# A decoder's grouped-query cross attention on one core: running maxima held in bf16, column sums and three of fifteen key tiles of a pass multiplied as bf16 halves

## The reference, cut to what matters

```python
q = rope(rms_norm((x @ Wq.T).reshape(b, 256, 16, 128)))
kv_in = concat([context, x], axis=1)                      # 1857 rows
k = rope(rms_norm((kv_in @ Wk.T).reshape(b, 1857, 4, 128)))
v = (kv_in @ Wv.T).reshape(b, 1857, 4, 128)
scores = einsum('bhqd,bhkd->bhqk', q, repeat(k, 4)) * 128 ** -0.5
attn = einsum('bhqk,bhkd->bhqd', softmax(scores), repeat(v, 4))
x = x + attn.reshape(b, 256, 2048) @ Wo.T
```

## Time and profile before

| what | value |
|---|---|
| median of three runs | 1650.81 us (1650.22 to 1650.82) |
| the profiled execution | 1648.11 us, its span 1646.3 us |
| PE busy | 1470.2 us (89%), 8223 matmuls |
| DVE busy | 1287.7 us (78%) |
| POOL busy | 1127.9 us (69%) |
| ACT busy | 1029.3 us (63%) |
| mean granted TensorE clock | 0.966 of full speed |

### The profile page before, as it was taken

The page is one execution under the profiler, slowest core; times in us unless marked ns, Lnnn a source line. Parts: engine busy times, 40 slices in busy tenths (PEclk is TensorE's granted clock), DMA queues, the critical chain, the costliest instruction groups (busy, mean ns, idle before and its releaser), DMA issues. The chain is left out here.

```text
span 1646.3 us, 25844 instructions
## 1 busy us (share of the span) xinstructions
PE 1470.2 (89%) x8223; PEld 855.8 (52%) x8332; DVE 1287.7 (78%) x2581; ACT 1029.3 (63%) x2439; POOL 1127.9 (69%) x1033
## 2 busy tenths in 40 slices
PE   6598697757778999999999999989999999999988
PEld 5477365533544555455455555545545555554455
DVE  7876577878569888787977888887887878878766
ACT  3364464744366777676677766676776766766552
POOL 2363471112459789988978998888898878877742
PEclk9799798979899999999999999999999999999999
DMA  3000831020000001000000100000000000000020
GB/s 102 1 2 2 296 114 39 1 73 0 32 1 14 14 1 41 14 1 1 1 1 1 28 14 1 1 1 1 14 28 1 1 1 1 1 1 1 1 59 26
DMA packets 30991, 38.47 MB, mean 23 GB/s; under 512 B 4996, under 2 KB 26504, under 8 KB 30856
## 3 DMA queue, kind: packets, MB, share of 16 engines
q1 hardware_dynamic: 30856, 36.82, 6.9%
HBM read 35.76 MB, written 1.05 MB: 22 GB/s over the span
## 5 line engine op out<-in xcount | busy, mean ns | idle before, releaser
L2168 POOL TENSOR_TENSOR stream_acc<-stream_acc,stream_weights 128x512 f32<-128x512 f32 (+1 forms) x374 | 491.9, 1315 | 80.6 <-ACT stream_weights L2059 59.0
L1988 PE MATMUL stream_banks<-stream_weights,stream_v 128*128 128x512 f32 (+1 forms) x876 | 451.6, 600 | 0.0
L2240 DVE TENSOR_TENSOR stream_most<-stream_most,stream_banks 128x512 f32<-128x512 f32 (+1 forms) x416 | 284.9, 685 | 157.4 <-ACT stream_weights L2053 142.2
L2053 ACT COPY stream_weights<-stream_banks 128x512 f32<-128x512 f32 (+1 forms) x438 | 256.6, 586 | 238.8 <-PE stream_banks L1956 231.0
L2059 ACT ACTIVATE stream_weights<-stream_weights 128x512 f32<-128x512 f32 (+1 forms) x438 | 278.5, 637 | 60.2 <-DVE stream_weights L2226 57.6
L2226 DVE TENSOR_TENSOR stream_weights<-stream_weights,stream_banks 128x512 f32<-128x512 f32 (+1 forms) x438 | 297.0, 680 | 2.8 <-PE stream_banks L1977 1.5
L2175 POOL TENSOR_TENSOR stream_by_cos<-stream_by_cos,stream_by_sin 128x256 f32<-128x256 f32 x192 | 135.8, 728 | 88.4 <-DVE stream_by_sin L2282 88.2
L1956 PE MATMUL stream_banks<-stream_q_t_lo,stream_k_t_hi 128*128 128x512 bf16 (+1 forms) x479 | 181.7, 379 | 9.2 <-DVE stream_most L2240 3.1
L1956 PE MATMUL stream_banks<-stream_q_t_hi,stream_k_t_lo 128*128 128x512 bf16 (+1 forms) x480 | 182.1, 379 | 0.1
L1956 PE MATMUL stream_banks<-stream_q_t_hi,stream_k_t_hi 128*128 128x512 bf16 (+1 forms) x388 | 147.6, 381 | 15.5 <-DVE stream_most L2240 14.8
L1988 PEld LDWEIGHTS stream_banks<-stream_weights,stream_v 128*128 128x128 f32 (+1 forms) x876 | 144.0, 191 | 29.7 <-issue 5.3
(11 more groups left out here) (445 smaller groups left out, 3099.6 us busy)
## 6 DMA issues: line engine op xcount, KB each, us to landing
memory_raw_t<-in_ctx_t SPq DMA_DIRECT2D x4, 1601.0 KB, 9.1
memory_raw<-in_ctx SPq DMA_DIRECT2D x4, 1536.0 KB
row_ctx_t<-in_ctx_t SPq DMA_DIRECT2D x6, 512.0 KB, 3.7
early_raw<-in_L_xattn_Wq SPq DMA_DIRECT2D x4, 512.0 KB, 3.8
early_raw<-in_L_xattn_Wo SPq DMA_DIRECT2D x4, 512.0 KB, 3.9
row_ctx_t<-in_ctx_t SPq DMA_DIRECT2D x1, 1601.0 KB, 7.0
moe_raw_up<-in_L_ffn_wi SPq DMA_DIRECT2D x6, 256.0 KB, 4.3
model_x<-in_x SPq DMA_DIRECT2D x1, 1024.0 KB, 5.4
```

The source lines that it names most:

```text
L1988: nc.tensor.matmul(ps[:, 2 + n, :], v[0:r, g % 2, t, :], room(step)[0:r], start=(t == 0), stop=(t == KT - 1)).then_inc(weighed, 1)
L2053: nc.scalar.copy(room(step)[0:r], ps[0:r, step % 2, :]).then_inc(copied, 1)
L2168: nc.gpsimd.tensor_tensor(acc[0:r, h % 2, :], acc[0:r, h % 2, :], room(step)[0:r], ALU.add).then_inc(acc_ready, 1)
L2240: nc.vector.tensor_tensor(most[0:r], most[0:r], ps[0:r, step % 2, :], ALU.max).then_inc(maxed, 1)
```

## The change

The maxima, the exponentials, the sums and the rest stay where they are; what differs:

- `most` is bf16, and PE turns it with bf16 transposes into the first half of bank 6 read as bf16.
- `turn_top`, `flatten`, `own` and its DMA are gone. In slot 1, after `lower`, DVE makes `tops`, the bf16 identity times `top` (`place_top`, 128x512), and in slot 2 PE spreads it with one bf16 product of 512 columns against an array of -1 (`less`).
- Column sums: in slot 6 ACT casts `acc` to a bf16 half, DVE subtracts it to make the other (`split_high`, `split_low`, into `halves`, part of the array `raw`), and PE makes eight bf16 products of one column in slot 7 instead of eight f32 records in slot 6. The last pass keeps the f32 way.
- Key tiles 5, 10 and 14: 19 slots after its scores the exponentiated tile is split in the same way into the same two `halves`, and 20 slots after `weigh` makes three bf16 products of halves of v and p. v of these tiles is kept as two bf16 halves in the room of the f32 tile; ACT writes the one, DVE the other.
- A split waits until PE has used the split before it. In a slot DVE makes `split_low` after `keep_most`, and ACT makes `split_high` after `exponent`.
- `raw` is shared, so Wo is loaded in eight parts of 256 KB, the context chunks 2 and 3 being issued behind parts 5 and 6.

```diff
-TOPS_LATE, FLAT_LATE, SPREAD_LATE = STEPS, STEPS + 1, STEPS + 2
+TOPS_LATE, SPREAD_LATE = STEPS, STEPS + 2
 SUM_LATE = ATT_LATE + 1
+SPLIT_LATE = SUM_LATE
+SPLIT_TILES = (5, 10, 14)
+def sums_in(slot):
+    return [h for h in pass_at(slot, SUM_LATE + 1) if h < PASSES - 1] + [h for h in pass_at(slot, SUM_LATE) if h == PASSES - 1]
+def splits_in(slot):
+    found = [("sum", h) for h in pass_at(slot, SPLIT_LATE) if h < PASSES - 1]
+    step = slot - LOWER - 1
+    if 0 <= step < ALL and step % STEPS in SPLIT_TILES:
+        found.append(("tile", step))
+    return found
...
-        most = sb("most", [P, HALF])
+        most = sb("most", [P, HALF], BF16)
+        tops = sb("tops", [P, 4, P], BF16)
+        turned_most = ps[:, 6, :].bitcast(BF16)[:, 0:HALF]
+        raw_o = raw[:, 0:512].rearrange("p (h n) -> p h n", h=2)
+        halves = [raw[:, 512 + 256 * i:768 + 256 * i].bitcast(BF16) for i in range(2)]
...
                 def out_weights(k):
                     if k >= 1:
-                        sp.wait_ge(wo_lo, 2 * k)
+                        sp.wait_ge(wo_lo, k)
...
-                        last = nc.tensor.transpose(ps[:, 6, c * P:(c + 1) * P], most[:, c * P:(c + 1) * P], const["ident"][:])
+                        last = nc.tensor.transpose(turned_most[:, c * P:(c + 1) * P], most[:, c * P:(c + 1) * P], const["ident_b"][:])
-                def turn_top(h):
-                    pe.wait_ge(top_ready, h + 1)
-                    wait_bank6("flat", h)
-                    nc.tensor.matmul(ps[0:4, 6, 0:P], top[:], const["ident_b"][:], start=True, stop=True).then_inc(top_turned, 1)
                 def spread(h):
-                    pe.wait_ge(flat_ready, h + 1)
+                    pe.wait_ge(tops_ready, h + 1)
...
-                    for c in range(4):
-                        last = nc.tensor.matmul(ps[:, 7, c * P:(c + 1) * P], own[:, c, :], flat, start=True, stop=True)
-                    last.then_inc(spread_ready, 1)
+                    nc.tensor.matmul(ps[:, 7, :], less[:], tops[:].rearrange("p c n -> p (c n)"), start=True, stop=True).then_inc(spread_ready, 1)
...
+                    if t in SPLIT_TILES:
+                        if n == 0:
+                            pe.wait_ge(taken, part_at[(UNITS * g + QT + t // 4, t % 4 // 2)] + 1)
+                        pe.wait_ge(split_lo, split_at["tile", step] + 1)
+                        for one, two in ((0, 0), (0, 1), (1, 0)):
+                            last = nc.tensor.matmul(ps[:, 2 + n, :], value_halves(g, t)[one][0:r], halves[two][0:r],
+                                                    start=False, stop=(t == KT - 1 and one == 1))
+                        last.then_inc(weighed, 1)
+                        return
...
-                        pe.wait_ge(acc_ready, after_first(STEPS * (h + 1) - 1))
+                        pe.wait_ge(split_lo, split_at["sum", h] + 1)
                         for c in range(4):
-                            last = nc.tensor.matmul(ps[:, 6, c:c + 1], acc[:, h % 2, c * P:(c + 1) * P], ones[:], start=True, stop=True)
+                            for part in range(2):
+                                last = nc.tensor.matmul(ps[:, 6, c:c + 1], halves[part][:, c * P:(c + 1) * P], ones_b[:],
+                                                        start=(part == 0), stop=(part == 1))
...
+                def split_high(kind, n):
+                    if kind == "sum":
+                        ac.wait_ge(acc_ready, after_first(STEPS * (n + 1) - 1))
+                    else:
+                        ac.wait_ge(p_ready, n + 1)
...
+                    nc.scalar.copy(split_part(kind, n, 0), split_source(kind, n)).then_inc(split_hi, 1)
...
+                def place_top(h):
+                    ve.wait_ge(top_ready, h + 1)
+                    if h >= 1:
+                        ve.wait_ge(spread_ready, h)
+                    nc.vector.tensor_tensor(tops[:], bcast(const["ident_b"][:], 1, 4), bcast(top[:], 2, P), ALU.mult).then_inc(tops_ready, 1)
...
+                def split_low(kind, n):
+                    ve.wait_ge(split_hi, split_at[kind, n] + 1)
+                    nc.vector.tensor_tensor(split_part(kind, n, 1), split_source(kind, n), split_part(kind, n, 0), ALU.subtract).then_inc(split_lo, 1)
```

More of the change, by code:

```diff
@@ L1843, in cross_stream @@
         for s in SLOTS:
-            for kind, items in (("tops", pass_at(s, TOPS_LATE)), ("flat", pass_at(s, FLAT_LATE)), ("turn", turns_in(s)),
-                                ("sum", pass_at(s, SUM_LATE)), ("out", outs_in(s))):
+            for kind, items in (("tops", pass_at(s, TOPS_LATE)), ("turn", turns_in(s)),
+                                ("sum", sums_in(s)), ("out", outs_in(s))):
                 for item in items:
@@ L2028, in _ @@
                         turn_most(h)
[L2029 to L2030 removed]
                     for u in turns_in(slot):
                         turn(u)
[L2033 removed]
+                    for h in sums_in(slot):
                         sum_up(h)
@@ L2084, in take_values @@
                         ac.wait_ge(weighed, STEPS * (HALVES * (g - 2) + 1) + tiles.stop)
-                    nc.scalar.copy(v[:, g % 2, tiles.start:tiles.stop, :], projected_values(u, n)).then_inc(v_taken, 1)
+                    plain = [t for t in tiles if t not in SPLIT_TILES]
+                    for t in tiles:
+                        if t in SPLIT_TILES:
+                            last = nc.scalar.copy(value_halves(g, t)[0], projected_values(u, n)[:, t - tiles.start, :])
+                    if plain:
+                        last = nc.scalar.copy(v[:, g % 2, plain[0]:plain[-1] + 1, :],
+                                              projected_values(u, n)[:, plain[0] - tiles.start:plain[-1] + 1 - tiles.start, :])
+                    last.then_inc(v_taken, 1)
                 def high(u):
@@ L2113, in _ @@
                         exponent(slot - LOWER)
+                    for kind, n in splits_in(slot):
+                        split_high(kind, n)
                     for h in pass_at(slot, ATT_LATE):
@@ L2126, in _ @@
                             vary(u, 1)
-                    for h in pass_at(slot, FLAT_LATE):
-                        flatten(h)
                     for u in turns_in(slot):
@@ L2319, in _ @@
                         lower(slot - LOWER)
+                    for h in pass_at(slot, TOPS_LATE + 1):
+                        place_top(h)
                     for h in pass_at(slot, ATT_LATE + 1):
@@ L2330, in _ @@
                         keep_most(slot)
+                    for kind, n in splits_in(slot):
+                        split_low(kind, n)
                     if 0 <= slot - WEIGH < ALL:
                         accumulate_rest(slot - WEIGH)
-                    for h in pass_at(slot, SUM_LATE):
+                    for h in sums_in(slot):
                         invert(h)
```

81 lines of the change are left out of this document (44 added, 37 removed).

## The result

The changed kernel takes **1751.95 us** (median, 1749.73 to 1754.25) against 1650.78 (1650.22 to 1650.82) of the kernel before, run beside it: **1.0614 times as long**, 95% interval 1.0595 to 1.0632. The forecast had the sign; its +26 us are +101, outside the range of 1625 to 1702. The profiled execution has a span of 1751.4 us against 1646.3, so the two traces hold 105.1 us of difference.

What follows compares the result with a forecast made beforehand. PE was taken to bound plain passes, DVE and POOL the long ones. Plain pairs +1.3 us (+21 in all), long passes +6, start and end −1 on 1648.1 gave 1674, as median 1677; range 1655 to 1702 for this case, 1625 to 1702 overall.

Steps and rivals of the forecast that it cites:

- W: Time one split_low holds DVE: 0.6 to 1.6 us, taken as 1.0, and as 1.2 for the even pass's sum split.
- Sum split, even pass, +2.4: Even pass: PE waits for the sum's low half, so slot 8's scores start 2.4 us later; bounds 1.8 to 2.8.
- odd pass, +0.3: Odd pass: the sum's split makes slot 8 start 0.3 us later; bounds 0 and 0.9.
- some 3: Even pass: PE, reaching the sums at about 1295.1, stands some 3 us waiting for the split.
- What a wait costs: Sum splits in plain passes: PE's wait was charged as the delay to slot 8, 2.4 us even and 0.3 odd.
- The renewing passes, "1.3 each, +6": Five long passes renewing context and rotation tables: 1.3 us added to each (five POOL waits at 0.3), +6 in all.
- Tile splits, "0.5 a pair": Tile splits in slots 3, 9 and 14: delay add_out and the second Wo projection, 0.5 us a pair; bounds 0 and 2.
- 12.5 free: DVE in a plain pair: 12.5 us free of 67.3, in 16 pieces, against ten added instructions of 10 us.
- Start and end, "−1": Stage start and last pass: constant's wait and cast, turn_top and flatten go, three splits come; −1 us together.
- PE's saving, 1.30 a pass: PE's cheaper weigh, turning, turn_top and sums save 1.30 us a pass, 42 in 32, if PE stayed the bound everywhere.
- The saving arrives: Rival: quicker bf16 maxima free DVE about 4 us a pass, so no wait at the sums; 1626 us; chance 0.25.
- POOL becomes the bound: Rival: POOL pays 1.0 us per added DVE instruction, even passes stretch some 1 us; 1700 us; chance 0.10.

Runs made afterwards that it cites:

- kernel 3: Changed kernel without the tile splits: all fifteen tiles weighed in f32, sums from bf16 halves kept; 1709.2 us, 1.0361.
- Kernel 1: Changed kernel with the row sums taken as before, in f32 in slot 6 without a split; tile splits and bf16 maxima kept; 1688.9 us, 1.0238.
- experiment 4: Changed kernel with twelve more bf16 products on PE in even passes, ahead of its wait for the sum's low half; 1736.4 us, 1.0526.
- kernel 5: Changed kernel with only the maxima's part (bf16 maxima and turning, place_top, single spread product); sums and all tiles f32, Wo in eight parts; 1640.5 us, 0.9948.
- experiment 6: kernel 5 plus ACT and DVE making the halves for tiles 5, 10 and 14, which nobody reads; 1693.4 us, 1.0266.
- experiments 3 and 7: 3 made kernel 3; 7 is kernel 5 plus ACT and DVE making halves of the sum in slot 6 that nobody reads, 1643.2 us, 0.9969.

## Why the prediction was wrong in size

By its own steps, with what was measured:

- **W, DVE's time for a split: right on average, wrong where it was used.** The 87 tile splits take 1.00 us by record on average. But the sum's split, for which 1.2 stood, takes 0.69 by record in all eight plain even passes, and DVE's next instruction starts 0.60 after it (1370.51 to 1371.11), the lower bound. In kernel 3, without tile splits, it takes 1.35 in all eight.
- **Sum split, even pass, +2.4; odd pass, +0.3: right, in part by luck.** Kernel 1 differs from the changed kernel in the sums alone: most of its plain even passes take 32.3 us and its shortest odd ones 33.95, against 34.5 and 34.52 with the halves at full clock, so +2.2 and +0.6. PE's wait was 2.76 to 2.96 us for "some 3". The luck: W at half of what stood and eight products at 0.20 for 0.48 would have made it less, but DVE's maximum of slot 6 came only 0.33 us earlier in the pass, where the savings that the forecast has ahead of it are 0.76.
- **What a wait costs: the step that failed first.** The sum priced a wait as the time that PE stands. Behind it PE ran at 1.2 GHz for 3.4 us or more, in five of eight plain even passes and in every renewing one; experiment 4 shows the cause. Some 24 to 35 us of the 105 (estimate), and nothing in the range for it.
- **The renewing passes, "1.3 each, +6": the step that failed most.** They are six, and cost +42.6. I had written that DVE and POOL have nothing free there, and then charged only POOL's waits, instead of DVE's four splits and `place_top` (5 x 1.0, less what it had free) plus the waits that they make. (Five waits at 0.3 are also 1.5, not 1.3.) By kernel 5 the maxima's part with `place_top` costs 4.9 of it, by experiment 6 the tiles' splits 14.4, by experiments 3 and 7 the sums' reading 21.7.
- **Tile splits, "0.5 a pair", saving 0.63 a pass on PE: wrong sign for the part.** The product itself is as forecast: three bf16 products 0.65 from start to start (785.16 to 785.80). But the splits' load alone costs 1.1 us in a plain pair (31.55 + 34.49 became 32.62 + 34.49) and up to 3.1 in another (passes 4 and 5), 53 in all. In the changed kernel's plain even pass the excess over the forecast lies in slots 10 to 12, where PE waits 0.50 us for a tile's half and 0.44 for the Wo projection's bank (rows below), and in slot 2, 0.4 ahead of `spread`: 1.3 us for the 0.5. The total of 10 us in "12.5 free" was the wrong test: PE waits wherever DVE is late for the next score, lowering or rotation, and what is free elsewhere doesn't give that back.
- **Start and end, "−1": wrong.** The last pass and the rest cost +18.4. In the last pass DVE also takes a share of the sums (before as after); in the changed kernel PE waits 10.0 us in 8 for the tiles' halves from 1598 us on, and unread halves alone cost 12.2 there.
- **PE's saving, 1.30 a pass: too low.** Turning `most` 0.23 for 0.24 (784.93 to 785.16), right. The eight sum products take **0.20** (1371.34 to 1371.54), where 0.48 was used and 0.1 to 0.8 allowed: 0.6 saved, not 0.33. `turn_top`, put at 0.15, saves 0.35: slot 1 takes 1.86 with it (1282.88 to 1284.74) and 1.50 without (1408.69 to 1410.19 in kernel 5), because the `weigh` behind it also takes longer, 0.97 for 0.86. `spread` was put at nothing and saves 0.2 in odd passes: before, its four products hold PE 0.33 and the `weigh` ahead of them runs 0.95 instead of 0.86. Together that is 0.57 to 0.72 a pass in kernel 5 for 0.34. By the load price of the Trainium skill (TensorE: Matmul & The Clock Gate, LDWEIGHTS) eight loads of 128 columns would be an estimated 0.85 us; 0.20 decides against it for loads that stand behind one another like these. In the trace one load of 128 bf16 columns ahead of a score takes 0.10 by record, and the eight together 0.28: they overlap.
- **The rivals.** "The saving arrives" failed as argued: a maximum with a bf16 output takes 681 ns (685 before). "POOL becomes the bound" failed: POOL is busy 67% of the span and waits 54 us for DVE's rotations between 700 and 1600 us.

The kernel before, for `turn_top` and `spread`:

```profile
1284.74 0.38 PE L1956 MATMUL stream_banks<-stream_q_t_hi,stream_k_t_hi 128*128 128x512 bf16 x1
...
1318.15 1.02 PE L1988 MATMUL stream_banks<-stream_weights,stream_v 128*128 128x512 f32 x2
1319.10 0.39 PE L1977 MATMUL stream_banks<-row_ctx_t,cross_own 4*128 4x128 bf16 x4
1319.43 0.39 PE L1956 MATMUL stream_banks<-stream_q_t_hi,stream_k_t_hi 128*128 128x512 bf16 x1
```

The changed kernel: waits of PE in slots 10 and 11 of an even pass at full clock, the sums' loads, and then the turning and the tile's product of an odd pass:

```profile
773.94 0.81 PE L2018 MATMUL stream_banks<-early_raw,stream_v 128*128 128x512 bf16 x3 [0.50 <-DVE early_raw L2347]
...
775.84 0.28 PE L2053 MATMUL stream_banks<-cross_w_o_hi,stream_att_hi 128*128 128x256 bf16 x1 [0.44 <-DVE model_x L2368]
```

```profile
1371.31 0.28 PEld L2031 LDWEIGHTS stream_banks<-cross_ones_b,early_raw 128*128 128x128 bf16 x8 [3.42 <-issue]
```

```profile
784.93 0.39 PE L1996 MATMUL stream_banks<-model_ident_b,stream_most 128*128 128x128 bf16 x4
785.16 0.81 PE L2018 MATMUL stream_banks<-early_raw,stream_v 128*128 128x512 bf16 x3
785.80 0.38 PE L1988 MATMUL stream_banks<-stream_q_t_hi,stream_k_t_hi 128*128 128x512 bf16 x1
```

## What to carry to other kernels

Work that is moved from a full engine to one with 20% free is not free: list the slots in which the second engine has under one such instruction to spare, and charge each of them, and each stage in which the first already waits for it, with the whole instruction. Charge a wait of PE with what it does to the clock as well: here 1.6 us behind five of eight waits of 3 us in plain even passes. Before reading a result of another engine in a new place, time the kernel with that work done and not read: the difference between load (tiles: 53 us; sums: 3) and wait (sums: 66) says whether to remove work or to move the reader.

## What the runs showed of the hardware

More work made the kernel faster: 12 products in front of a wait in each of 16 passes, some −15 us, with clock 1.00 in place of 0.95 in the pass shown. And eight bf16 products of one column with a 128x128 load each take 0.20 us from the first's start to the next instruction, 0.025 each; the f32 ones took 0.81 for four (eight records).
